# A graph layer and a state-space block on one core: the decay matrix from two single-pass products, a copy and a normalisation moved to ScalarE

## The chip, the cores and the metric

The kernel runs on one core of a Trainium2 chip. The core has five engines that run side by side and meet only through semaphores: TensorE (PE, matrix products; PEld is its loading of weights), VectorE (DVE), ScalarE (ACT), GpSimd (POOL) and SyncE (SP, which issues the DMAs here). The metric is the device time of one execution in microseconds. Three runs of the kernel before gave 901.51, 902.1 and 906.42 us; 902.1 is the median.

## The reference, cut to what matters

The input is x (4096 rows of 128) with an adjacency matrix of 4096 x 4096. A graph layer comes first: a masked softmax over the neighbours, two products with it, and a residual. Then a state-space block runs over the 4096 rows in 32 chunks of 128 rows, with 4 heads:

```python
x = x + _L0_gnn_ref(_layernorm(x), h0, a, temp, adj, 1)
x = x + _L0_ffn_ref(_layernorm(x)[None], W_in, conv_w, ...)[0]
# inside the block
z, xBC, dt = jnp.split(x @ W_in, ...)
xBC = jax.nn.silu(conv)                        # 4 taps, 384 channels
xh, Bmat, Cmat = jnp.split(xBC, [256, 320])    # B and C: 64 channels each
dt = jax.nn.softplus(dt + dt_bias);  A = -jnp.exp(A_log)
dA = dtc * A                                   # one number per row and head
Lmat = jnp.exp(segsum(dA))                     # decay matrix, 128 x 128 per head
Y_diag = jnp.einsum('bcln,bcsn,bhcls,bcshp->bclhp', Cc, Bc, Lmat, xdt)
...
Y = Y * jax.nn.silu(z);  Y = Y * rsqrt(mean(Y * Y) + EPS) * norm_w
out = (Y @ W_out) @ W_lin + b_lin
```

The change is about three values in it: the sums of dA inside the exponential of Lmat, the matrix C, and the layernorm in front of the block.

## The kernel before, in words

The program has two halves. The first reads the adjacency matrix, turns it into codes of one byte, makes two 0/1 masks of it (mask A on ScalarE, mask C on VectorE) and multiplies them with Y on TensorE. The second half reads the codes back, makes the masks again for the second product, and runs the state-space block beside it. The functions named slot below are that second half.

There is one slot function for each engine, and schedule calls it 37 times: 32 row tiles and 5 more calls in which the pipeline runs empty. In slot s an engine works on five different tiles at once. ok[0] is the end of the graph layer for tile s-1 and its layernorm, ok[1] the input projection and the convolution of tile s-2, ok[2] the decay matrix of tile s-3, ok[3] the outputs and the state of tile s-4, and ok[4] the storing of tile s-5. The order within an engine is the order of the code; across engines only the semaphores count. A helper named link lets an engine wait for its own last instruction before it goes on.

What the lines do, in the second half:
- VectorE: L691 is a pass that makes mask C from codes, four in each slot (mask(0) to mask(3)). L838 and L852 make the mixing matrix, L858 the output row tile (it waits for rs_ready, from GpSimd's L592), L862 and L867 the tile x1 after the graph layer, L880 and L905 its mean and variance. L895 are the nine convolution taps, between which the small steps of the softplus stand. L912 is the layernorm itself (normalise2), L921, L924 and L930 read the products of the state step, L967 gives dA to GpSimd, L976, L982 and L985 are the gates, and L986 makes a second copy of C, moved to partitions 0 to 63.
- GpSimd: L562 and L563 add epsilon and take the power -0.5 for the layernorm. L566 and L542 to L550 are six instructions of 128x128 on residuals. L573 multiplies the triangle upto with dA, which gives dam (128 x 4 x 128). L581, L583 and L585 scale x and the state. L591 and L592 are epsilon and power for the last norm, rs_ready.
- TensorE: L1283 and L1293 are the products with the masks, eight instructions of 256 columns each in a block. L1421 multiplies the triangle after with dam, 512 columns in fp32; after is exactly 0 or 1. L1377 transposes the normalised tile.
- ScalarE: L1053 makes mask A, L1072 reads the accumulator, L1152 copies the turned tile, L1165 are the first products of the convolution, L1183 is the tanh of it.

## Time and profile before

| | |
|---|---|
| runs, us | 901.51, 902.1, 906.42 |
| the profiled execution, us | 900.56 |
| its span, first to last instruction, us | 898.8 |
| mean granted TensorE clock | 0.957 |
| busy: PE, PEld, DVE | 818.9 (91%), 767.0 (85%), 792.5 (88%) |
| busy: ACT, POOL | 592.0 (66%), 543.9 (61%) |

The profiled execution took 900.56 us; its span is 898.8 us. Busy times are sums over the whole span, while the two halves have different limits, so they don't tell which engine sets the length of a slot. A slot is read from the distance between two executions of the same line. An instruction's time in the profile includes time in which it stands at its engine's head for something that is no semaphore.

### The profile page before, as it was taken

What the parts mean: (1) busy time and instruction counts of PE and PEld (TensorE: products, weight loads), DVE (VectorE), ACT (ScalarE), POOL (GpSimd) and SP (SyncE); (2) the same over time, 40 slices, a digit from 0 to 9 for tenths busy, and PEclk for the clock granted to TensorE, in tenths of its full rate; (3) what the DMA queues carried; (4) which work ended last, traced back from release to release, by engine and by line L of the source; (5) the groups of instructions that cost most, each with busy time, mean ns of one, the idle gap of its engine ahead of it and who ended that gap; (6) DMA issues with size and microseconds to landing.
All of it is one profiled execution on the core that took longest, in us unless ns stands there. A gap on an engine that the chain in (4) does not pass through costs nothing.

```text
span 898.8 us, 21768 instructions
## 1 busy us (share of the span) xinstructions
PE 818.9 (91%) x6650; PEld 767.0 (85%) x6650; DVE 792.5 (88%) x1968; ACT 592.0 (66%) x1026; POOL 543.9 (61%) x1123
## 2 busy tenths in 40 slices
PE   3978999989998999955889999999999999999976
PEld 1668999989998999954889999999999999999954
DVE  6567999989998999657699999999999999999983
ACT  6676877778787887533566666666666666666641
POOL 4462556664655666788656666575665756666642
PEclk9878999999999999995899999999999999999997
DMA  6456978878696967700111112111121111110000
GB/s 190 141 187 196 286 254 267 266 215 280 206 306 195 308 206 258 224 3 24 36 60 62 50 50 66 36 61 58 38 64 35 61 58 41 61 36 16 7 7 10
DMA packets 97545, 110.72 MB, mean 123 GB/s; under 512 B 6464, under 2 KB 89280, under 8 KB 97472
## 3 DMA queue, kind: packets, MB, share of 16 engines
q1 hardware_dynamic: 97472, 109.74, 38.7%
q8 instruction: 46, 0.75, 0.4%
q14 instruction: 27, 0.22, 0.1%
HBM read 90.85 MB, written 18.87 MB: 122 GB/s over the span
## 4 chain that ended last, share of the span: by engine, by line
PE 40%; POOL 20%; issue 13%; DVE 12%; ACT 8%; DMA 5%; POOLq 1%; DVEq 1%; ACTq 0%; SPq 0%
PE accA L1283 12%; PE accC L1293 11%; DMA adj_in<-in_adj_dram 5%; ACT edges L1006 3%; PE ps L1223 3%; PE ps L1421 2%; DVE maskC L691 2%; PE ps L1401 2%; PE ps L1399 2%; ACT maskA L1053 2%; DVE code L683 2%; POOL small L471 2%; DVE code L895 1%; PE ps L1403 1%; POOL featsum L490 1%
## 5 line engine op out<-in xcount | busy, mean ns | idle before, releaser
L1283 PE MATMUL accA<-Y,maskA 128*128 128x260 f32 (+1 forms) x2048 | 313.8, 296 | 30.5 <-DVE Y L662 19.1
L1053 ACT ACTIVATE maskA<-code 128x1024 fp32r<-128x1024 int8 x256 | 269.3, 1053 | 56.6 <-PE accC L1293 28.3
L1283 PEld LDWEIGHTS accA<-Y,maskA 128*128 128x128 f32 x2048 | 270.0, 193 | 33.7 <-ACT maskA L1053 16.9
L1293 PE MATMUL accC<-Y,maskC 128*128 128x260 f32 (+1 forms) x2048 | 295.3, 288 | 1.1 <-DVE maskC L691 1.1
L1293 PEld LDWEIGHTS accC<-Y,maskC 128*128 128x128 f32 x2048 | 268.4, 194 | 1.4 <-DVE maskC L691 1.4
L683 DVE SCALAR_TENSOR_TENSOR code<-f_rows,neg_f,ps 128x512 int8<-128x512 f32 x256 | 178.4, 740 | 37.1 <-PE ps L1223 35.5
L691 DVE TENSOR_SCALAR maskC<-code 128x1024 fp32r<-128x1024 int8 x256 | 210.0, 824 | 1.2 <-issue 0.3
L1006 ACT ACTIVATE edges<-adj_in 128x1024 bf16<-128x1024 f32 x128 | 133.1, 1044 | 24.5 <-DMA adj_in<-in_adj_dram 16.4
L895 DVE SCALAR_TENSOR_TENSOR code<-adj_in,f_rows,code 128x128 f32<-128x128 f32 x288 | 113.7, 415 | 0.0
L1223 PE MATMUL ps<-ident,edges 128*128 128x128 bf16 x1024 | 82.5, 225 | 13.3 <-ACT edges L1006 9.8
L1223 PEld LDWEIGHTS ps<-ident,edges 128*128 128x128 bf16 x1024 | 60.7, 101 | 24.1 <-DVE code L683 8.0
L562 POOL TENSOR_TENSOR f_rows<-f_rows,consts 128x1 f32<-128x1 f32 x32 | 8.4, 263 | 118.6 <-DVE f_rows L905 118.6
L573 POOL TENSOR_TENSOR f_rows<-f_rows 128x512 f32<-128x512 f32 x32 | 39.1, 1220 | 31.6 <-DVE f_rows L967 30.4
L462 POOL COPY small<-roww 128x2 f32 (+1 forms) x32 | 6.3, 198 | 83.2 <-DVE ps_sum L709 81.4
L1201 ACT COPY adj_in<-ps 128x256 f32<-128x256 f32 x32 | 12.0, 375 | 49.6 <-PE ps L1433 49.6
L1160 ACT COPY code<-ps 128x260 f32<-128x260 f32 x32 | 12.0, 376 | 48.7 <-PE ps L1388 48.7
L1183 ACT ACTIVATE code<-code 128x384 f32<-128x384 f32 x32 | 16.8, 525 | 35.6 <-DVE code L895 35.6
L1165 ACT ACTIVATE code<-ps,f_rows 128x128 f32<-128x128 f32 x96 | 37.5, 474 | 0.0
L581 POOL TENSOR_TENSOR adj_in<-code,f_rows 128x256 f32<-128x256 f32 x32 | 32.2, 1006 | 7.2 <-ACT code L1190 7.2
L1401 PE MATMUL ps<-adj_in,code 128*128 128x64 f32 x256 | 36.5, 266 | 0.0
L1421 PE MATMUL ps<-f_rows 128*128 128x512 f32 x64 | 36.0, 646 | 0.0
L1399 PE MATMUL ps<-adj_in,code 128*128 128x128 f32 x128 | 30.0, 317 | 6.2 <-DVE code L852 5.4
(201 smaller groups left out, 1487.3 us busy)
## 6 DMA issues: line engine op xcount, KB each, us to landing
adj_in<-in_adj_dram SPq DMA_DIRECT2D x128, 512.0 KB, 4.6
edge_codes<-code SPq DMA_DIRECT2D x8, 2048.0 KB, 10.0
code<-edge_codes SPq DMA_DIRECT2D x32, 512.0 KB, 3.3
xn<-in_x_dram SPq DMA_DIRECT2D x4, 512.0 KB, 5.8
adj_in<-in_x_dram SPq DMA_DIRECT2D x32, 64.0 KB, 1.8
adj_in<-in_L_gnn_h_dram SPq DMA_DIRECT2D x32, 64.0 KB, 1.9
out_dram<-adj_in SPq DMA_DIRECT2D x32, 64.0 KB, 1.6
f_rows<-in_L_ffn_W_in_dram SPq DMA_DIRECT2D x1, 192.0 KB, 6.6
```

Of the source, the lines that this page charges most:

```text
L573: g.tensor_tensor(dam, upto.unsqueeze(1).broadcast_to([P, NH, P]), tiny[:, 2 + k % 2, NH:2 * NH].unsqueeze(2).broadcast_to([P, NH, P]), AL ...
L683: v.scalar_tensor_tensor(out=code[:, par, :, jt * P:(jt + 1) * P], in0=f1_rows[:, rows].rearrange("p (i r) -> p i r", i=IT), scalar=neg_f2 ...
L691: v.tensor_scalar(maskC[:, b % MASKS], src, 2.0, None, ALU.is_equal).then_inc(S["maskC_ready"], 1)
L895: ins = v.scalar_tensor_tensor(out=conv[:, cb], in0=hist[:, k2, cb, tap:tap + P], scalar=conv_wt[:, cb, tap:tap + 1], in1=conv[:, cb], op0 ...
L1006: s.activation(edges[:, h % 4], adj_in[:, h % 4], ACT.Sign).then_inc(S["signed"], 1)
L1053: s.activation(maskA[:, b % MASKS], src, ACT.Relu, bias=-2.0).then_inc(S["maskA_ready"], 1)
L1223: m = t_.matmul(ps[jt % TRB][:, it * P:(it + 1) * P], edges[:, b % 4, it, j * P:(j + 1) * P], ident2[:], start=True, stop=True)
L1283: t_.matmul(accA[k][:, 0:2 * cols], maskA[:, b % MASKS, l * P:(l + 1) * P], Y[:, jt, 0, :, 0:cols], start=jt == 0, stop=jt == NT - 1)
L1293: m = t_.matmul(accC[k][:, 0:2 * cols], maskC[:, b % MASKS, l * P:(l + 1) * P], Y[:, jt, 1, :, 0:cols], start=jt == 0, stop=jt == NT - 1)
L1399: t_.matmul(ps[0][:, kb * P:(kb + 1) * P], xbc[:, (k - 4) % 2, kb, :], skip_w[:, kb], start=True, stop=False)
L1401: t_.matmul(ps[0][:, h * HD:(h + 1) * HD], wmix[:, h], xdt[:, h * HD:(h + 1) * HD], start=False, stop=h == (kb + 1) * P // HD - 1)
L1421: t_.matmul(ps[3][:, 0:NH * P], after, dam.rearrange("p h w -> p (h w)"), start=True, stop=True)
```

## The change

Four edits:
1. The decay matrix. dA = dt * A is split on GpSimd into a part that is rounded to fp32r and the rest. dam becomes two matrices of 4 x 128 columns, written by one instruction of 1024 elements, of type fp32r. TensorE sums two fp32r products of 512 columns in place of one fp32 product of 512. The matrices lie in the room that the tile edges of the first half had.
2. The second copy of C is made on ScalarE, from the finished xbc at the head of the next slot, in place of VectorE's L986. TensorE's product with it waits for the new semaphore cT_ready.
3. The layernorm in front of the block is one activation on ScalarE behind mask(2), x * rstd + bias, in place of VectorE's L912.
4. GpSimd makes the bias for it, -mean * rstd, in one more instruction, with a link ahead.

```diff
--- before.py
+++ after.py
@@ -66,7 +66,9 @@
             return ctx.enter_context(nc.psum_tensor(name, shape, dt))
 
         adj_in = sb("adj_in", [P, 4, IT, JH * P])
-        edges = sb("edges", [P, 4, IT, 2 * P], BF16)
+        with nc.sbuf_tensor("edges", [P, 4, IT, 2 * P], BF16) as edges:
+            pass
+        edge_room = sb("edge_room", [P, 4 * IT * P], F32R)
         code = sb("code", [P, 2, IT, NT * P], I8)
         maskA = sb("maskA", [P, MASKS, JB * P], F32R)
         maskC = sb("maskC", [P, MASKS, JB * P], F32R)
...
@@ -186,7 +188,9 @@
         ztan = y_space.take(DI)
         cT = rows_space.take(2, P)
         gate = rows_space.take(2, DI)
-        dam = rows_space.take(NH, P)
+        dam = edge_space.take(2, NH, P)
+        after = edge_space.take(P)
+        da_parts = edge_space.take(2, NH)
         expD = code_space.take(NH, P)
         gm = adj_space.take(P)
         wmix = code_space.take(NH, P)
...
@@ -560,7 +564,8 @@
                     wait(pool, "ln_done", s_)
                     wait(pool, "xn2_ready", s_ - 1)
                     link(g.tensor_tensor(tiny[:, 1, 0:1], tiny[:, 0, 1:2], consts[:, 2, 0:1], ALU.add))
-                    g.tensor_tensor(tiny[:, 1, 1:2], tiny[:, 1, 0:1], consts[:, 0, 0:1], ALU.pow).then_inc(S["rstd2"], 1)
+                    link(g.tensor_tensor(tiny[:, 1, 1:2], tiny[:, 1, 0:1], consts[:, 0, 0:1], ALU.pow))
+                    g.tensor_scalar(tiny[:, 1, 2:3], tiny[:, 0, 0:1], tiny[:, 1, 1:2], -1.0, ALU.mult, ALU.mult).then_inc(S["rstd2"], 1)
 
                     wait(pool, "out_done", s_ - 4)
                     g.tensor_tensor(x1b[:, kt], x1[:, kt % 2], b_row, ALU.add).then_inc(S["x1b_done"], 1)
...
@@ -570,8 +575,12 @@
 
                     wait(pool, "dt_ready", s_ - 1)
                     wait(pool, "p_cum", s_ - 2)
-                    g.tensor_tensor(dam, upto.unsqueeze(1).broadcast_to([P, NH, P]),
-                                    tiny[:, 2 + k % 2, NH:2 * NH].unsqueeze(2).broadcast_to([P, NH, P]), ALU.mult).then_inc(S["dam_ready"], 1)
+                    da = tiny[:, 2 + k % 2, NH:2 * NH]
+                    link(g.tensor_tensor(da_parts[:, 0], tiny[:, 2 + k % 2, 0:NH], a_row, ALU.mult))
+                    link(g.tensor_tensor(da_parts[:, 1], da, da_parts[:, 0].bitcast(F32), ALU.subtract))
+                    g.tensor_tensor(dam.rearrange("p a h w -> p (a h) w"), upto.unsqueeze(1).broadcast_to([P, 2 * NH, P]),
+                                    da_parts.rearrange("p a h -> p (a h)").bitcast(F32).unsqueeze(2).broadcast_to([P, 2 * NH, P]),
+                                    ALU.mult).then_inc(S["dam_ready"], 1)
                 if ok[2]:
 
                     kc = (k - 3) % 2
...
@@ -904,13 +913,6 @@
                     dve.wait_ge(S["vch"], seen)
                     v.bn_aggr(tiny[:, 0, 0:2], tiny[:, 7, 0:6]).then_inc(S["ln_done"], 1)
 
-                def normalise2():
-
-                    if ok[0]:
-                        dve.wait_ge(S["rstd2"], s_)
-                        wait(dve, "p_xT", s_ - 2)
-                        v.tensor_scalar(xn2[:, kt], x1[:, kt], tiny[:, 0, 0:1], tiny[:, 1, 1:2], ALU.subtract, ALU.mult).then_inc(S["xn2_ready"], 1)
-
                 summed_y = [0]
 
                 def y_state():
...
@@ -982,9 +982,8 @@
                     v.scalar_tensor_tensor(out=gate[:, k2], in0=ztan, scalar=1.0, in1=zdt[:, 0:DI], op0=ALU.add, op1=ALU.mult).then_inc(S["gate_done"], 1)
                     dve.wait_ge(S["ctan_ready"], s_ - 1)
                     wait(dve, "p_y", s_ - 3)
-                    v.scalar_tensor_tensor(out=xbc[:, k2], in0=gate_t, scalar=1.0, in1=conv, op0=ALU.add, op1=ALU.mult)
-                    v.scalar_tensor_tensor(out=cT[0:DS, k2], in0=gate_t[DS:P, CB - 1], scalar=1.0, in1=conv[DS:P, CB - 1], op0=ALU.add,
-                                           op1=ALU.mult).then_inc(S["conv_ready"], 1)
+                    wait(dve, "cT_ready", s_ - 3)
+                    v.scalar_tensor_tensor(out=xbc[:, k2], in0=gate_t, scalar=1.0, in1=conv, op0=ALU.add, op1=ALU.mult).then_inc(S["conv_ready"], 1)
                 mask(3)
                 end_chain()
 
...
@@ -1145,6 +1144,11 @@
 
                 if ok[0]:
                     read_acc(s_ - 1, (k - 1) % 2, F, 1)
+                if ok[2]:
+
+                    act.wait_ge(S["conv_ready"], s_ - 2)
+                    wait(act, "p_y", s_ - 4)
+                    s.copy(cT[0:DS, (k - 3) % 2], xbc[DS:P, (k - 3) % 2, CB - 1]).then_inc(S["cT_ready"], 1)
                 if ok[1]:
 
                     act.wait_ge(S["p_xT"], s_ - 1)
...
@@ -1177,6 +1181,10 @@
                     act.wait_ge(S["zcopy"], s_ - 1)
                     s.activation(ztan, zdt[:, 0:DI], ACT.Tanh).then_inc(S["zt_ready"], 1)
                 mask(2)
+                if ok[0]:
+                    act.wait_ge(S["rstd2"], s_)
+                    wait(act, "p_xT", s_ - 2)
+                    s.activation(xn2[:, (k - 1) % 2], x1[:, (k - 1) % 2], ACT.Identity, bias=tiny[:, 1, 2:3], scale=tiny[:, 1, 1:2]).then_inc(S["xn2_ready"], 1)
                 if ok[1]:
                     act.wait_ge(S["conv_pre"], s_ - 1)
                     wait(act, "conv_ready", s_ - 2)
...
@@ -1418,7 +1426,8 @@
                     pe.wait_ge(S["conv_ready"], s_ - 2)
                     t_.matmul(ps[2][:, 0:NH], upto, da, start=True, stop=True)
                     t_.matmul(ps[2][:, NH:2 * NH], ones[:], da, start=True, stop=True)
-                    t_.matmul(ps[3][:, 0:NH * P], after, dam.rearrange("p h w -> p (h w)"), start=True, stop=True)
+                    for half in range(2):
+                        t_.matmul(ps[3][:, 0:NH * P], after, dam[:, half].rearrange("p h w -> p (h w)"), start=half == 0, stop=half == 1)
                     for cb in range(CB):
                         m = t_.transpose(ps[2][:, (cb + 1) * P:(cb + 2) * P], xbc[:, c3, cb], ident[:])
                     m.then_inc(S["p_cum"], 1)
...
@@ -1437,6 +1446,7 @@
                 if ok[2]:
 
                     pe.wait_ge(S["conv_ready"], s_ - 2)
+                    pe.wait_ge(S["cT_ready"], s_ - 2)
                     if ok[3]:
                         pe.wait_ge(S["st_done"], s_ - 3)
                     t_.matmul(ps[1][:, 0:P], xbc[:, (k - 3) % 2, CB - 1, :], cT[:, (k - 3) % 2], start=True, stop=True).then_inc(S["p_g"], 1)
```

GpSimd's order around the decay matrix in a full slot, before (edge_room is the new room, f_rows holds upto, dA and other small tiles):

```order
L550 TENSOR_TENSOR adj_in<-featw 128x128
L573 TENSOR_TENSOR f_rows<-f_rows 128x512
L581 TENSOR_TENSOR adj_in<-code,f_rows 128x256
L583 TENSOR_TENSOR f_rows<-adj_in,code 128x256
L585 TENSOR_TENSOR ywork<-code,f_rows 64x256
L591 TENSOR_TENSOR f_rows<-f_rows,consts 128x1
L592 TENSOR_TENSOR f_rows<-f_rows,consts 128x1
L392 ISA
L562 TENSOR_TENSOR f_rows<-f_rows,consts 128x1
L563 TENSOR_TENSOR f_rows<-f_rows,consts 128x1
L566 TENSOR_TENSOR adj_in<-adj_in,f_rows 128x128
```

The same place of GpSimd in the changed file:

```order
L554 TENSOR_TENSOR adj_in<-featw 128x128
L579 TENSOR_TENSOR edge_room<-f_rows 128x4
L580 TENSOR_TENSOR edge_room<-f_rows,edge_room 128x4
L581 TENSOR_TENSOR edge_room<-f_rows,edge_room 128x1024
L590 TENSOR_TENSOR adj_in<-code,f_rows 128x256
L592 TENSOR_TENSOR f_rows<-adj_in,code 128x256
L594 TENSOR_TENSOR ywork<-code,f_rows 64x256
L600 TENSOR_TENSOR f_rows<-f_rows,consts 128x1
L601 TENSOR_TENSOR f_rows<-f_rows,consts 128x1
```

Two small instructions stand ahead of the matrix now, and it is twice as wide; what follows it keeps its order (L581 to L592 are now L590 to L601). The instruction L568, behind the power, is the one of edit 4.

VectorE's order from the last small step of the softplus to the end of the slot, before:

```order
L958 TENSOR_TENSOR f_rows<-f_rows 128x4
L912 TENSOR_SCALAR adj_in<-adj_in,f_rows 128x128
L921 TENSOR_TENSOR ywork<-ps,f_rows 128x256
L924 TENSOR_TENSOR code<-ywork,ps 64x256
L964 SCALAR_TENSOR_TENSOR f_rows<-f_rows 128x4
L930 TENSOR_TENSOR ywork<-ywork,ps 128x256
L967 TENSOR_TENSOR f_rows<-f_rows 128x4
L976 TENSOR_TENSOR f_rows<-ywork,f_rows 128x256
L691 TENSOR_SCALAR maskC<-code 128x1024
L982 SCALAR_TENSOR_TENSOR f_rows<-ywork,code 128x256
L985 SCALAR_TENSOR_TENSOR code<-code 128x384
L986 SCALAR_TENSOR_TENSOR f_rows<-code 64x128
```

The same place of VectorE in the changed file:

```order
L960 TENSOR_TENSOR f_rows<-f_rows 128x4
L923 TENSOR_TENSOR ywork<-ps,f_rows 128x256
L926 TENSOR_TENSOR code<-ywork,ps 64x256
L965 SCALAR_TENSOR_TENSOR f_rows<-f_rows 128x4
L932 TENSOR_TENSOR ywork<-ywork,ps 128x256
L968 TENSOR_TENSOR f_rows<-f_rows 128x4
L976 TENSOR_TENSOR f_rows<-ywork,f_rows 128x256
L700 TENSOR_SCALAR maskC<-code 128x1024
L982 SCALAR_TENSOR_TENSOR f_rows<-ywork,code 128x256
L986 SCALAR_TENSOR_TENSOR code<-code 128x384
L700 TENSOR_SCALAR maskC<-code 128x1024
```

The layernorm and the copy of C are gone from it, and all else stands as before. L858 of the kernel before is L867 in the changed file.

## Rows read from the trace of the kernel before

**Rows 1.** Busy us by stage: engines with instruction counts, granted clock, DMA share, GB/s.

```profile
300.00:400.00 100.00, 93.27 (x869) 91.02 (x867) 79.98 (x148) 65.69 (x73) 68.27 (x187) 1.00 0.62 196
600.00:700.00 100.00, 99.49 (x765) 93.29 (x764) 98.46 (x282) 65.14 (x151) 63.13 (x109) 1.00 0.17 54
```

**Rows 2.** VectorE in order of time, one slot: start, duration, line, operation, idle.

```profile
610.72 0.18 DVE L905 BATCH_NORM_AGGREGATE f_rows<-f_rows 128x2 f32<-128x6 f32 x1
...
614.36 0.52 DVE L912 TENSOR_SCALAR adj_in<-adj_in,f_rows 128x128 f32<-128x128 f32 x1
...
616.32 1.54 DVE L691 TENSOR_SCALAR maskC<-code 128x1024 fp32r<-128x1024 int8 x1
617.78 0.83 DVE L982 SCALAR_TENSOR_TENSOR f_rows<-ywork,code 128x256 f32<-128x256 f32 x1
618.53 0.97 DVE L985 SCALAR_TENSOR_TENSOR code<-code 128x384 f32<-128x384 f32 x1
619.51 0.61 DVE L986 SCALAR_TENSOR_TENSOR f_rows<-code 64x128 f32<-64x128 f32 x1
620.15 0.69 DVE L691 TENSOR_SCALAR maskC<-code 128x1024 fp32r<-128x1024 int8 x1
...
622.55 0.34 DVE L858 SCALAR_TENSOR_TENSOR adj_in<-ps,f_rows,adj_in 128x128 f32<-128x128 f32 x1
...
624.63 0.17 DVE L905 BATCH_NORM_AGGREGATE f_rows<-f_rows 128x2 f32<-128x6 f32 x1
```

**Rows 3.** GpSimd in order of time, same slot.

```profile
610.97 0.28 POOL L562 TENSOR_TENSOR f_rows<-f_rows,consts 128x1 f32<-128x1 f32 x1 [3.64 <-DVE f_rows L905]
611.33 0.55 POOL L563 TENSOR_TENSOR f_rows<-f_rows,consts 128x1 f32<-128x1 f32 x1
...
616.09 1.22 POOL L573 TENSOR_TENSOR f_rows<-f_rows 128x512 f32<-128x512 f32 x1 [0.75 <-DVE f_rows L967]
617.27 1.06 POOL L581 TENSOR_TENSOR adj_in<-code,f_rows 128x256 f32<-128x256 f32 x1
...
620.25 1.00 POOL L592 TENSOR_TENSOR f_rows<-f_rows,consts 128x1 f32<-128x1 f32 x1
624.89 0.28 POOL L562 TENSOR_TENSOR f_rows<-f_rows,consts 128x1 f32<-128x1 f32 x1 [3.64 <-DVE f_rows L905]
```

**Rows 4.** GpSimd in order of time: first and last of 26 slots, one later row.

```profile
495.07 1.01 POOL L592 TENSOR_TENSOR f_rows<-f_rows,consts 128x1 f32<-128x1 f32 x1
...
842.83 1.00 POOL L592 TENSOR_TENSOR f_rows<-f_rows,consts 128x1 f32<-128x1 f32 x1
...
887.12 0.62 POOL L581 TENSOR_TENSOR adj_in<-code,f_rows 128x256 f32<-128x256 f32 x1 [7.18 <-ACT code L1190]
```

**Rows 5.** Waits between 560 and 860 us: who for whom, total, times, longest.

```profile
POOL f_rows L562 <- DVE f_rows L905: 79.5, 22, 3.8
...
ACT code L1183 <- DVE code L895: 22.4, 21, 2.0
POOL f_rows L573 <- DVE f_rows L967: 16.9, 22, 0.8
```

**Rows 6.** VectorE in order of time, an early slot.

```profile
452.44 1.26 DVE L982 SCALAR_TENSOR_TENSOR f_rows<-ywork,code 128x256 f32<-128x256 f32 x1
453.62 0.54 DVE L985 SCALAR_TENSOR_TENSOR code<-code 128x384 f32<-128x384 f32 x1
```

**Rows 7.** TensorE in order of time, same slot as rows 2.

```profile
612.76 1.11 PE L1421 MATMUL ps<-f_rows 128*128 128x512 f32 x2
...
613.95 1.20 PE L1283 MATMUL accA<-Y,maskA 128*128 128x256 f32 x8
```

**Rows 8.** ScalarE's groups by form, whole span: count, busy, mean ns, idle before.

```profile
L1165 ACT ACTIVATE code<-ps,f_rows 128x128 f32<-128x128 f32 x96 | 37.5, 474 | 0.0
```

**Rows 9.** GpSimd's groups by form, whole span.

```profile
L433 POOL TENSOR_TENSOR Y<-code,Y 128x1024 fp32r<-128x1024 f32 x2 | 4.7, 2355 | 2.6 <-ACT Y L1042 2.6
L501 POOL TENSOR_TENSOR ywork<-xn,colw 128x1024 f32<-128x1024 f32 x1 | 1.9, 1900 | 0.4 <-POOL row_out L484 0.4
```

More of the change, by code:

```diff
@@ L146, in gnn_ffn_kernel @@
         y_space = Space(ywork[:, :])
+        edge_space = Space(edge_room[:, :])
         DI = W_out.shape[0]
@@ L169, in gnn_ffn_kernel @@
         upto = rows_space.take(P)
-        after = rows_space.take(P)
         x_in = adj_space.take(2, F)
@@ L217, in gnn_ffn_kernel @@
             mix_ready xdt_ready  ps_ready y_read yg_ready st_done skip_ready yT_ready ssq_ready rs_ready
-            exp_done out_done zcopy""".split()
+            exp_done out_done zcopy cT_ready""".split()
         S = {n: sem(n) for n in names}
@@ L958, in slot @@
                     last = step(v.tensor_tensor(p, horner[:, 2, :, 5], si, ALU.mult))
-                    normalise2()
                     y_state()
@@ L968, in slot @@
                 else:
-                    normalise2()
                     y_state()
```

## The prediction

> **What bounds the kernel now.** I first read the table by stage. In the second half of the program (the state-space block beside the second products) TensorE is busy 99.49 of 100 us and VectorE 98.46, while GpSimd shows 63.13; in the first half TensorE has 93.27 and VectorE 79.98 [rows 1]. The change touches nothing in the first half, so everything below is about the slots of the second. Their length is the distance of two equal instructions: L905 at 610.72 and 624.63 on VectorE, L562 at 610.97 and 624.89 on GpSimd [rows 2, 3], so 13.92 us. There are 26 such full slots: L592 runs from 495.07 to 842.83 in 26 executions, 25 distances of 13.91 [rows 4].
>
> Then I read the order in time of one slot on each engine, because three engines are near the limit and GpSimd, with 63% busy, looks free but is not. Every slot holds a loop: L905 (statistics of the new row tile) releases GpSimd's L562; GpSimd works through to L592, the norm factor of an older tile; L592 releases VectorE's L858, and from L858 VectorE goes on, in its own order, to the next L905. In numbers: L905 ends at 610.90, L592 ends at 621.25, L858 starts at 622.55 and the next L905 ends at 624.80 [rows 2, 3]. So GpSimd's part is 10.35 us (0.75 of it is L573 waiting for VectorE's step size L967), the slack between L592 and L858 is 1.30, and VectorE's part is 2.25. GpSimd's 3.64 us of idle time before L562 are not free time: 2.25 + 0.10 of them are this loop's VectorE part, and only 1.30 is slack. The list of waits says the same: 79.5 us over 22 slots are L562 waiting for L905, and 16.9 are L573 waiting for L967 [rows 5].
>
> The third reading is that VectorE and GpSimd take turns. A mask pass L691 takes 0.69 us at 620.15 but 1.54 at 616.32, where it ends 0.55 after L573 (0.55 being most of a pass) [rows 2, 3]. L982 takes 0.83 beside L581, and 1.26 in an early slot; L985 takes 0.97 in the full slot, and 0.54 where GpSimd stands still [rows 2, 6]. The other way round, L581 takes 1.06 behind the mask pass and 0.62 without it [rows 3, 4], and the power L592 takes 1.00 behind the mask pass of 620.15, while the same power in L563 takes 0.55. Each of these is explained by one engine standing for the other's whole instruction and then running at its normal speed. The Trainium skill (SBUF — State Buffer, "Who interferes with whom") states this: GpSimd shares a port pair with VectorE, as an exclusive lock held for a whole instruction, against VectorE instructions with two SBUF inputs or in a two-port mode. The trace agrees, by the 1.54 against 0.69. By that rule of the Trainium skill a longer GpSimd instruction is paid on both engines, which speaks against this change: without turns the slot would be rival 1's 13.4, with them it is what is worked out below from rows.
>
> **The change part by part.**
> TensorE: L1421's product goes from fp32 to two fp32r products of 512 columns. L1421 now shows two records and 1.11 us; eight fp32r products of 256 columns take 1.20 [rows 7], so two of 512 cost as much as four of those, 0.60 at most. Removed: 0.5 us per slot. TensorE alone would then allow a slot of 13.4.
>
> VectorE: L912 (0.52) and L986 (0.61) go [rows 2]; instructions overlap by 0.08, so 1.0 to 1.05 us. But by the next part some of this is waiting for GpSimd, which what stands behind them would do in their place; I take 0.6 as sure.
>
> ScalarE: gets a copy of 64x128 and an activation of 128x128. The nearest row, L912 on VectorE, has 0.52 for the latter; ScalarE does its conv activations L1165, of the same size, in a mean of 0.47 [rows 8]. Together at most 1.0 us on an engine that is 65% busy [rows 1]; L1183 alone waits 22.4 us in 21 slots [rows 5], and the activation is placed just ahead of it. Cost 0 while that second is there; without it at most 0.5. The normalised tile is wanted by TensorE only at the head of the next slot, and the copy of C most of a slot after it is made, so both new waits are covered. Behind the copy's wait in ScalarE's queue stands the copy of the turned tile; it may be 0.5 late, and its taker, TensorE, has by then gained that.
>
> GpSimd, per slot:
> - L568 in the changed file, 128x1, with a link ahead of it: L562 of that size takes 0.28, and 0.36 from start to start [rows 3]. I take 0.3.
> - two 128x4 instructions with links ahead of the matrix: 0.3 each by the same row, 0.6.
> - the matrix from 512 to 1024 elements. 1.22 now [rows 3]. A 1024 element instruction with one spread operand took 1.90; one with two full operands and an fp32r output 2.36 [rows 9]. So it grows by 0.68 to 1.14; I take 0.9, as the rows with spread operands are nearer in form and the 1.22 holds a short wait for L976.
> - the 0.75 us wait for L967 is used up: the step size comes some 0.4 earlier (L912 is gone) and GpSimd 0.3 later.
> Sum: 10.35 - 0.75 + 0.3 + 0.6 + 0.9 = 11.4 us. The room up to L858 is 11.65. So with the turns as they are, the loop would not bind at all, by 0.25.
>
> The turns are what decides. Now GpSimd stands for VectorE about 1.4 us per slot: 0.44 in L581, 0.45 in L592, the rest in L573 and L585. Going through the slot with the rule "whoever asks first holds for its whole instruction", and the undisturbed times 0.69, 0.54, 0.62, 0.55 and 1.90, I let the new instructions come at their new places: L568 shifts GpSimd's five small row instructions against the convolution taps L895, the two 128x4 instructions each meet the mask pass L691 or L982, and L581, L583, L585 come one mask pass later. That gives 0.5 to 1.0 us of waits more than now. With 0.75 the GpSimd part is 12.15, so L858 starts 0.5 later than now: a slot of 14.4 us. VectorE then idles ahead of L858 and TensorE about 1.0 us per slot. TensorE's clock should stay: in a stretch with 93.27% busy the granted clock was 1.00 [rows 1].
>
> Early slots gain (VectorE and TensorE bind them), by at most 0.5 each for three slots; the last slots, where nothing runs beside the block, lose about as much in GpSimd's longer stretch. I put them at 0. Total: 26 x 0.5 = +13 us on a profiled time of 900.56 (span 898.8), so 913.6; the median of the runs is 902.1, 1.5 above the profiled one, so **915**.
>
> **The rivals.**
> 1. Turns cost nothing more, or VectorE's gain absorbs them. For it: 11.4 is under 11.65. Then VectorE (13.92 - 0.6) and TensorE (13.4) bind, a slot of 13.4 to 13.5: 26 x -0.48 = -12.5, **889.5**. Against it: three more instructions have to take turns.
> 2. Slack and new waits cancel, slot 13.8 to 14.05: **902**, within 4 us.
> 3. The GpSimd loop binds harder: the matrix at the 2.36 of rows 9 and 1.0 us of waits or more, slot 14.9 to 15.2: about 26 x 1.25, **934**. Its place is L858 waiting for L592; it decides from a GpSimd part of 12.6.
> 4. The split product isn't cheap: if fp32r products of 512 columns cost what the fp32 ones do, TensorE gets +0.94 or more per slot, slot 14.9, +24, **926**. Against it: the rate of the eight products in rows 7.
>
> **How the numbers follow.** Forecast (slot 14.2 to 14.8) 0.48, its own range 908 to 924; rival 1 0.27; rival 2 0.12; rival 3 0.10; rival 4 0.03. A measurement here can tell 0.5%, 4.5 us, from no change. Slower: 0.48 + 0.10 + 0.03 = 0.61; same 0.12; faster 0.27. The range 889 to 928 leaves out most of rival 3 and the edge of rival 1.
>
> **What would show it.** Right: VectorE's L858 (L867 in the changed file) waits for GpSimd's power in every full slot, 0.3 to 1.4 us, where it now starts 1.30 behind it; slots of 14.2 to 14.8; TensorE below 97% in the second half; the matrix at 1.9 to 2.4 us; VectorE's instructions beside it up to 2 us long. ScalarE's two additions wait for nobody that matters. Wrong: slots under 13.9 with L867 starting at once would mean that the turns were over-counted; slots over 15 that the matrix or the turns were under-counted; a wait of TensorE's L1385 or L1394 for ScalarE would mean that I wrongly costed the moved normalisation or copy at nothing.

## The result and the profile after

The changed kernel took 938.0 us (median of 4 runs, 937.16 to 939.79), the kernel before 902.88 beside it (4 runs, 901.51 to 906.42): 1.038 of it, interval 1.034 to 1.042. It is slower, as forecast, but by 35 us where 13 were forecast, and outside the range of 889 to 928. The span of its profiled execution is also 938.0 us (898.8 before), the mean granted clock there 0.940 (0.957). The two profiled executions lie 39 us apart, the medians 35.

The table by stage, with the columns of [rows 1]:

```profile
300.00:400.00 100.00, 95.65 (x892) 93.33 (x890) 80.74 (x150) 67.59 (x75) 69.05 (x188) 1.00 0.65 204
600.00:700.00 100.00, 90.93 (x706) 86.76 (x706) 82.86 (x234) 64.95 (x152) 75.96 (x118) 0.99 0.14 45
```

Between 300 and 400 us, in the first half, little changes. In the second, TensorE falls from 99.49 to 90.93 and VectorE from 98.46 to 82.86, and GpSimd rises from 63.13 to 75.96. The granted clock stays at the upper level there (0.99). One slot of the changed kernel on GpSimd, in order of time (start, duration, line, operation, idle time before and who ended it), answers to [rows 3]:

```profile
625.33 0.28 POOL L566 TENSOR_TENSOR f_rows<-f_rows,consts 128x1 f32<-128x1 f32 x1 [2.38 <-DVE f_rows L914]
625.69 0.55 POOL L567 TENSOR_TENSOR f_rows<-f_rows,consts 128x1 f32<-128x1 f32 x1
626.34 0.47 POOL L568 TENSOR_SCALAR f_rows<-f_rows 128x1 f32<-128x1 f32 x1
626.77 0.60 POOL L571 TENSOR_TENSOR adj_in<-adj_in,f_rows 128x128 f32<-128x128 f32 x1
...
630.37 0.79 POOL L554 TENSOR_TENSOR adj_in<-featw 128x128 f32<-128x128 f32 x1
631.40 0.57 POOL L579 TENSOR_TENSOR edge_room<-f_rows 128x4 fp32r<-128x4 f32 x1 [0.24 <-POOL adj_in L554]
632.05 0.52 POOL L580 TENSOR_TENSOR edge_room<-f_rows,edge_room 128x4 fp32r<-128x4 f32 x1
632.65 1.91 POOL L581 TENSOR_TENSOR edge_room<-f_rows,edge_room 128x1024 fp32r<-128x1024 f32 x1
634.52 1.06 POOL L590 TENSOR_TENSOR adj_in<-code,f_rows 128x256 f32<-128x256 f32 x1
...
637.40 0.55 POOL L601 TENSOR_TENSOR f_rows<-f_rows,consts 128x1 f32<-128x1 f32 x1
640.44 0.28 POOL L566 TENSOR_TENSOR f_rows<-f_rows,consts 128x1 f32<-128x1 f32 x1 [2.48 <-DVE f_rows L914]
```

VectorE in the same slot, answering to [rows 2]:

```profile
625.07 0.18 DVE L914 BATCH_NORM_AGGREGATE f_rows<-f_rows 128x2 f32<-128x6 f32 x1
...
633.32 1.79 DVE L861 TENSOR_TENSOR code<-code,adj_in 128x512 f32<-128x512 f32 x1
635.04 1.10 DVE L700 TENSOR_SCALAR maskC<-code 128x1024 fp32r<-128x1024 int8 x1
638.09 0.35 DVE L867 SCALAR_TENSOR_TENSOR adj_in<-ps,f_rows,adj_in 128x128 f32<-128x128 f32 x1 [1.96 <-POOL f_rows L601]
...
640.18 0.17 DVE L914 BATCH_NORM_AGGREGATE f_rows<-f_rows 128x2 f32<-128x6 f32 x1
```

The slot is 15.11 us here, 15.07 in the mean (13.91 before, counted in the same way: 25 distances of the power's line). All mean slots below are counted so. The output instruction L867 stands 1.96 us for GpSimd's power L601; before it started 1.30 behind it. From the start of the statistics to the end of that power it is 12.88 us (10.53 before): I call this the stretch. The waits between 560 and 860 us (who for whom: total, times, longest) say the same of all slots:

```profile
POOL f_rows L566 <- DVE f_rows L914: 49.5, 20, 2.7
DVE adj_in L867 <- POOL f_rows L601: 37.3, 20, 2.0
PEld ps L1407 <- issue: 27.4, 18, 1.6
```

GpSimd waits for VectorE and VectorE for GpSimd in every slot: the loop of the prediction now binds from both sides. The third line is TensorE standing ahead of the products with the mixing matrix. The profile names nobody for it; in the code they also wait for GpSimd's scaling L592, and in this slot they start at 636.71, 0.11 behind its end.

Who lost turns has changed as well. The nine convolution taps are one group in the page (line, operation, count | busy, mean ns | idle before); before the same group had 113.7 us in all and a mean of 415 ns:

```profile
L904 DVE SCALAR_TENSOR_TENSOR code<-adj_in,f_rows,code 128x128 f32<-128x128 f32 x288 | 91.6, 338 | 0.0
```

VectorE's taps no longer stand for GpSimd. GpSimd's row instructions (the seven of 128x128, L571 and L546 to L554 here) stand for VectorE instead, three at 0.60 and the last at 0.79 in the slot above.

Where the 39.2 us of span went: 26 full slots times 1.15 are 29.9; the ramp up and one more slot 3.1; the time from the last statistics (894.31, before 859.48) to the end grew from 39.3 to 43.7, 4.4; and the first statistics come 1.8 later.

Most of the 4.4 us at the end is TensorE's clock. From the transposes of the last tile (L1433 at 887.75, here L1442 at 923.72) to the end of the span it is 11.05 us before and 14.28 here, with the same work in it. The same product, first before, then after:

```profile
891.84 0.65 PE L1403 MATMUL ps<-code,f_rows 128*128 128x256 f32 x2
929.79 1.17 PE L1411 MATMUL ps<-code,f_rows 128*128 128x256 f32 x2
```

The granted clock is 1.00 from 890 to 896 us before (the upper level, 2.4 GHz) and 0.50 from 926 to 932 us here (1.2 GHz). Shortly ahead of this both show 0.50 (879 to 884 us before, 914 to 923 here); why it came back in the one and not in the other, no run here separates. In the last 12 us the profile of act_only shows 0.89, as the kernel before does (0.88), and the profiles of all other runs 0.50 to 0.64, so up to 3 us of their distance from the kernel before lie there and not in the slots.

### The profile page after: what moved, and what is told of

It reads as the page before. It is cut to its first block, busy times and chain, and to the rows that moved or that the text cites. A ratio compares the mean times of both kernels' runs of the same rounds, so it can differ in the third digit from the quotient of the medians.

```text
span 938.0 us, 21890 instructions
## 1 busy us (share of the span) xinstructions
PE 826.4 (88%) x6650; PEld 782.2 (83%) x6650; DVE 760.6 (81%) x1904; ACT 617.8 (66%) x1090; POOL 627.1 (67%) x1219
## 4 chain that ended last, share of the span: by engine, by line
POOL 41%; issue 18%; PE 17%; DVE 11%; ACT 6%; DMA 4%; POOLq 1%; DVEq 1%; ACTq 0%; SPq 0%
PE accA L1291 5%; PE accC L1301 5%; DMA adj_in<-in_adj_dram 3%; POOL adj_in L590 3%; POOL f_rows L592 3%; ACT edges L1005 3%; PE ps L1231 2%; POOL adj_in L554 2%; POOL small L475 2%; POOL ywork L594 2%; POOL adj_in L571 2%; DVE code L904 2%; POOL featw L547 2%; POOL featw L553 2%; POOL f_rows L567 2%
## 5 line engine op out<-in xcount | busy, mean ns | idle before, releaser
L1291 PE MATMUL accA<-Y,maskA 128*128 128x260 f32 (+1 forms) x2048 | 319.8, 300 | 29.9 <-DVE Y L671 18.2
L1291 PEld LDWEIGHTS accA<-Y,maskA 128*128 128x128 f32 x2048 | 275.5, 197 | 33.4 <-ACT maskA L1052 19.8
L1301 PEld LDWEIGHTS accC<-Y,maskC 128*128 128x128 f32 x2048 | 271.4, 196 | 1.6 <-DVE maskC L700 1.4
L700 DVE TENSOR_SCALAR maskC<-code 128x1024 fp32r<-128x1024 int8 x256 | 204.9, 805 | 0.3 <-issue 0.3
L904 DVE SCALAR_TENSOR_TENSOR code<-adj_in,f_rows,code 128x128 f32<-128x128 f32 x288 | 91.6, 338 | 0.0
L581 POOL TENSOR_TENSOR edge_room<-f_rows,edge_room 128x1024 fp32r<-128x1024 f32 x32 | 62.2, 1944 | 2.5
L1178 ACT ACTIVATE f_rows<-f_rows 128x4 f32<-128x4 f32 x32 | 6.6, 207 | 80.6 <-DVE f_rows L936 80.6
L1407 PEld LDWEIGHTS ps<-adj_in,code 128*128 128x128 f32 x128 | 21.1, 207 | 44.3 <-issue 42.9
L867 DVE SCALAR_TENSOR_TENSOR adj_in<-ps,f_rows,adj_in 128x128 f32<-128x128 f32 x32 | 11.2, 350 | 57.5 <-POOL f_rows L601 57.4
L861 DVE TENSOR_TENSOR code<-code,adj_in 128x512 f32<-128x512 f32 x32 | 51.2, 1601 | 0.1
```

What stands on the lines that cost most here:

```text
L581: g.tensor_tensor(dam.rearrange("p a h w -> p (a h) w"), upto.unsqueeze(1).broadcast_to([P, 2 * NH, P]), da_parts.rearrange("p a h -> p (a ...
L700: v.tensor_scalar(maskC[:, b % MASKS], src, 2.0, None, ALU.is_equal).then_inc(S["maskC_ready"], 1)
L861: v.tensor_tensor(wmix, expD, gm.unsqueeze(1).broadcast_to([P, NH, P]), ALU.mult).then_inc(S["mix_ready"], 1)
L904: ins = v.scalar_tensor_tensor(out=conv[:, cb], in0=hist[:, k2, cb, tap:tap + P], scalar=conv_wt[:, cb, tap:tap + 1], in1=conv[:, cb], op0 ...
L1291: t_.matmul(accA[k][:, 0:2 * cols], maskA[:, b % MASKS, l * P:(l + 1) * P], Y[:, jt, 0, :, 0:cols], start=jt == 0, stop=jt == NT - 1)
L1301: m = t_.matmul(accC[k][:, 0:2 * cols], maskC[:, b % MASKS, l * P:(l + 1) * P], Y[:, jt, 1, :, 0:cols], start=jt == 0, stop=jt == NT - 1)
```

## The experiments

The theory after the result: the loop through the wait for the power binds, and it is lengthened by the port turns that the added small GpSimd instructions (bias, two parts) cause, more than by the twice as wide matrix. (This last part did not hold for the time; see both_off.) Rivals: the matrix alone; ScalarE's additions; VectorE as the bound. All ratios are to the kernel before, from three rounds each, with the interval. Line numbers in rows are those of each run's own file; the order changes are written in short, not as code.

**One edit, or the others.** split_only is the kernel before with edit 1 alone:

```diff
+ link(g.tensor_tensor(da_parts[:, 0], tiny[:, 2 + k % 2, 0:NH], a_row, ALU.mult))
+ link(g.tensor_tensor(da_parts[:, 1], da, da_parts[:, 0].bitcast(F32), ALU.subtract))
- g.tensor_tensor(dam, ...)                        # 4 x 128
+ g.tensor_tensor(dam.rearrange(...), ...)         # 2 x 4 x 128, fp32r
```

> The kernel before with edit 1 alone (the split decay matrix: two 128x4 instructions, 1024 columns on GpSimd, two fp32r products). Theory L (the loop: GpSimd's stretch from VectorE's statistics to the power of the last norm, then VectorE's output instruction and back to the statistics, sets the slot): the stretch grows by 0.6 + 0.7 us and by turns, slot 14.6 to 15.2, 920 to 938 us. Rival S (what costs is on ScalarE: the moved copy and normalisation come late for TensorE): with these left out the time would fall below the kernel before, to some 890 us, by the cheaper products. Rival V (VectorE itself is slowed by the long GpSimd instruction, whatever waits for the power): also 920 to 940.

act_only is the changed kernel with these lines taken back (edits 2 to 4 alone).

> The changed kernel with edit 1 undone: copy of C and normalisation on ScalarE, the bias instruction on GpSimd, decay matrix as before (512 columns, one fp32 product). Theory L: GpSimd's stretch is about 11 us and fits the room, TensorE bounds with its old work, slot 13.9, 898 to 905 us. Rival S: keeps most of the loss, 925 to 938. Rival V: VectorE has 0.6 us less to do, but TensorE bounds, 898 to 905.

split_only: 924.22 us, 1.021 (1.017 to 1.025), slots of 14.53, stretch 12.37, a time within the expected 920 to 938. act_only: 900.95 us, 0.995 (0.992 to 0.998), slots of 13.94, stretch 11.75. Alone they are worth +2.1% and -0.5%, together +3.8%: they don't add. GpSimd in a slot of split_only:

```profile
610.84 0.46 POOL L554 TENSOR_TENSOR adj_in<-featw 128x128 f32<-128x128 f32 x1
612.05 0.37 POOL L578 TENSOR_TENSOR edge_room<-f_rows 128x4 fp32r<-128x4 f32 x1 [0.76 <-DVE f_rows L975]
...
617.90 1.13 POOL L600 TENSOR_TENSOR f_rows<-f_rows,consts 128x1 f32<-128x1 f32 x1
```

and VectorE's output instruction there, and in act_only:

```profile
619.07 0.35 DVE L866 SCALAR_TENSOR_TENSOR adj_in<-ps,f_rows,adj_in 128x128 f32<-128x128 f32 x1
```

```profile
623.26 0.35 DVE L859 SCALAR_TENSOR_TENSOR adj_in<-ps,f_rows,adj_in 128x128 f32<-128x128 f32 x1 [1.38 <-POOL f_rows L593]
```

In split_only the row part ends before the step size is there (it still waits 0.76 at L578), and the output follows directly behind the power: the edit alone used up all of the 1.30 of slack. act_only uses it up too, and waits. With both, the second user has no slack left. So act_only's time came true for another reason than the expected one (a stretch of about 11 that fits the room): the time was luck. Rival S is out by split_only, which has no addition on ScalarE and still loses 2.1%.

**The low half left out.** high_only keeps one part, a matrix of 512 and one product, so dA is only its rounded value:

```diff
- g.tensor_tensor(dam.rearrange("p a h w -> p (a h) w"), ...)
+ g.tensor_tensor(dam[:, 0], ...)
```

> The changed kernel with the low part of dA left out: one 128x4 instruction, a matrix of 512 fp32r columns, one fp32r product of 512 columns (so the decay matrix is computed from rounded values). Theory L: the stretch is shorter by 0.6 + 0.9 us, slot 13.6 to 14.1, 893 to 908 us. Rival V: about the same, 895 to 910. Rival S: 925 to 938, since nothing changes on ScalarE.

904.09 us, 0.998 (0.996 to 1.001), slots of 13.96, stretch 11.78, as expected by the loop and by rival V alike. The matrix took 1.37 (1.91 after). VectorE in one slot:

```profile
621.04 0.68 DVE L859 TENSOR_TENSOR code<-code,adj_in 128x512 f32<-128x512 f32 x1
...
624.71 0.35 DVE L865 SCALAR_TENSOR_TENSOR adj_in<-ps,f_rows,adj_in 128x128 f32<-128x128 f32 x1 [1.96 <-POOL f_rows L599]
```

The mixing matrix takes 0.68 here and 1.79 (L861) in the changed kernel, and yet the output waits the same 1.96: VectorE standing for GpSimd ahead of a wait costs nothing, it is only waited out at another place. The loop's length counts, and with 1.10 less of it the slot is 1.11 shorter.

**The matrix last.** dam_last is the changed kernel with GpSimd's order scalings (L590 to L594 of the changed kernel), norm (L600, L601), then the two parts and the matrix.

```diff
- if ok[1]: parts, matrix   if ok[2]: scalings   if ok[3]: norm
+ if ok[2]: scalings   if ok[3]: norm   if ok[1]: parts, matrix
```

> The changed kernel with one order changed on GpSimd: in each slot the scalings and the two instructions of the last norm come ahead of the decay matrix and its two small instructions, which then are the last of the slot. No instruction more or less. Theory L: the power is ready 3 us earlier, the output instruction waits for nothing, and the slot falls to what TensorE needs (13.4 to 13.7), 887 to 897 us. Rival V: VectorE meets the same GpSimd work, only elsewhere, 925 to 940. Rival G (GpSimd has too much work in all, in whatever order): 12.7 us of stretch plus turns, also at or above 14.5, 920 to 938.

910.13 us, 1.007 (1.004 to 1.009), slots of 14.12. That is 28 us better than the changed kernel, but not the 887 to 897 expected, and no gain over the kernel before. VectorE:

```profile
623.48 0.35 DVE L867 SCALAR_TENSOR_TENSOR adj_in<-ps,f_rows,adj_in 128x128 f32<-128x128 f32 x1 [0.54 <-POOL f_rows L591]
...
624.17 1.78 DVE L876 SCALAR_TENSOR_TENSOR adj_in<-ywork,row_out,adj_in 128x128 f32<-128x128 f32 x1
```

The wait is still 0.54, and now L876, in VectorE's own part of the loop, takes 1.78 instead of 0.35: it stands for the 1.93 us matrix. A wide GpSimd instruction moved off one half of the loop landed on the other. This is rival V's mechanism, though not its 925 to 940: the stretch fell to 10.47, and VectorE's part, from the output to the next statistics, rose from 2.1 to 3.5.

**One small instruction.** one_more is the kernel before with edit 4 alone; nobody reads the bias.

```diff
- g.tensor_tensor(tiny[:, 1, 1:2], ...pow).then_inc(S["rstd2"], 1)
+ link(g.tensor_tensor(tiny[:, 1, 1:2], ...pow))
+ g.tensor_scalar(tiny[:, 1, 2:3], ...).then_inc(S["rstd2"], 1)
```

> The kernel before with one more small instruction on GpSimd: the bias of the layernorm, 128x1, with a link ahead of it, and nobody reads it. Nothing else is changed. Theory F (it shifts GpSimd against VectorE's convolution taps, so that the turns flip): the six row instructions of 128x128 behind it take some 0.60 us each where they took 0.44 to 0.49, the taps 0.34 where they took 0.55, and the last of the six ends about 6.0 us after the statistics' start where it ended at 4.6. The time stays, 898 to 906 us, since GpSimd's stretch had 1.3 us of room. Rival P (it costs its own duration only): the last of the six ends at 5.1 to 5.3, taps stay at 0.55, time the same.

915.9 us, 1.015 (1.009 to 1.020), slots of 14.6 in the middle of the run, stretch 12.38. For the first row instructions and the taps the expectation came true (0.60, a mean of 340 ns), for the time not: something else was hit. GpSimd and VectorE at the same moment:

```profile
623.15 0.60 POOL L542 TENSOR_TENSOR featw<-xn,row_out 128x128 f32 x1
...
626.12 2.00 POOL L550 TENSOR_TENSOR adj_in<-featw 128x128 f32<-128x128 f32 x1
```

```profile
625.98 0.41 DVE L977 TENSOR_TENSOR f_rows<-ywork,f_rows 128x256 f32<-128x256 f32 x1
626.32 0.68 DVE L692 TENSOR_SCALAR maskC<-code 128x1024 fp32r<-128x1024 int8 x1
626.92 0.41 DVE L983 SCALAR_TENSOR_TENSOR f_rows<-ywork,code 128x256 f32<-128x256 f32 x1
627.25 0.54 DVE L986 SCALAR_TENSOR_TENSOR code<-code 128x384 f32<-128x384 f32 x1
```

L550 (0.46 for its like in split_only) takes 2.00, while four VectorE instructions in a row run at their undisturbed times (0.68 and 0.54 are those the prediction used). GpSimd lost the port to all of them. By the rule I had used, it would have had its turn behind the first.

This is where the time went. In the first three full slots of this run and in the last three L550 is done in 0.60:

```profile
524.56 0.60 POOL L550 TENSOR_TENSOR adj_in<-featw 128x128 f32<-128x128 f32 x1
```

There the added instruction is in place and the first row instructions take 0.60 as well, and yet these slots last 13.66 to 13.88 us, no more than the same slots of the kernel before (13.72 to 13.95). In the 20 slots between, L550 takes 2.00 and the slot 14.4 to 14.7. So where L550 was not held up, the added instruction and the turned row instructions cost nothing; what cost was the turns that L550 lost. In the changed kernel the like of it, L554, takes 0.79.

**The bias off GpSimd.** bias_on_scalar is the changed kernel with L568 replaced by two small activations on ScalarE:

```diff
- g.tensor_scalar(tiny[:, 1, 2:3], ...)
+ s.mul(tiny[:, 1, 3:4], tiny[:, 0, 0:1], tiny[:, 1, 1:2])
+ s.activation(tiny[:, 1, 2:3], tiny[:, 1, 3:4], ACT.Identity, scale=-1.0)
```

> The changed kernel with edit 4 taken off GpSimd: ScalarE makes the bias in two small activations ahead of the moved normalisation. Theory F: GpSimd's row instructions keep their old turns, the stretch up to the power is about 12.3 us as in the kernel with edit 1 alone, slot 14.4 to 14.6, 917 to 926 us. Rival P: the stretch is only 0.5 shorter at most, slot 14.7 to 14.9, 927 to 934. Rival S (ScalarE's additions are what costs): 938 or more.

918.06 us, 1.016 (1.011 to 1.022), slots of 14.33 to 14.55, stretch 12.2, as theory F expected. GpSimd's row instructions are back at 0.40 to 0.49, and the output waits 0.44. One instruction on 128x1 was worth 20 us of the 35.

**The parts off GpSimd too.** both_off also makes the two 128x4 parts on VectorE, ahead of dt_ready (`v.tensor_tensor(da_parts[:, 0], ...)` and the same for the rest). both_off_mid then puts the norm's two instructions directly behind the matrix, ahead of the scalings.

> The changed kernel with three small instructions taken off GpSimd: the bias made by ScalarE as in bias_on_scalar, and the two 128x4 parts of dA by VectorE. GpSimd keeps the matrix of 1024 columns. Theory L with F: the stretch is 11.1 to 11.4 us, slot 13.4 to 13.7, which TensorE or the loop sets, 887 to 899 us. Rival V (the wide matrix alone, in VectorE's way, is the cost): the slot stays over 14.3, 915 or more.

> both_off with GpSimd's two instructions of the last norm placed directly behind the matrix, ahead of the scalings. Theory L: the output instruction waits for nothing any more and TensorE or VectorE sets the slot, 13.4 to 13.6, 886 to 896 us. Rival T (the scalings now meet VectorE's x1 instructions, which are on the loop too, as the matrix did in dam_last): no gain over both_off, or up to 8 us more than it.

both_off: 922.06 us, 1.022 (1.016 to 1.027); slots of 14.46 though the stretch was 11.35 and nothing waited for the power. My theory failed and rival V came true: VectorE was the bound. VectorE, and its stage:

```profile
609.95 2.40 DVE L696 TENSOR_SCALAR maskC<-code 128x1024 fp32r<-128x1024 int8 x1
612.27 0.83 DVE L982 SCALAR_TENSOR_TENSOR f_rows<-ywork,code 128x256 f32<-128x256 f32 x1
613.03 0.97 DVE L986 SCALAR_TENSOR_TENSOR code<-code 128x384 f32<-128x384 f32 x1
613.92 1.10 DVE L696 TENSOR_SCALAR maskC<-code 128x1024 fp32r<-128x1024 int8 x1
```

```profile
600.00:700.00 100.00, 95.28 (x734) 90.47 (x735) 98.64 (x272) 72.13 (x174) 66.14 (x104) 1.00 0.16 50
```

The mask pass stands 1.71 for the matrix, the three behind it about 0.4 each for the scalings: these four rows alone hold 3.0 us of standing in each slot, which the 98.64 counts as busy. So the matrix is not the smaller cost. The small instructions lengthen the stretch more than it does (1.25 for the two parts against 0.69 for its growth), but taking all three off GpSimd gives back 16 us, while leaving out half the matrix and one of them (high_only) gives back 34. both_off_mid: 904.14 us, 1.001 (0.998 to 1.003), slots of 13.78: 18 us better than both_off, which rival T had excluded, but short of the 886 to 896 expected. The 2.40 stayed, the 0.83 and 0.97 became 0.41 and 0.55.

**The norm early, in both kernels.** rs_mid is the changed kernel, before_rs_mid the kernel before, each with the norm's two instructions behind the matrix:

```diff
- if ok[1]: matrix   if ok[2]: scalings   if ok[3]: norm
+ if ok[1]: matrix   if ok[3]: norm   if ok[2]: scalings
```

> The changed kernel with GpSimd's two instructions of the last norm placed behind the decay matrix and ahead of the three scalings, nothing else. Theory L (the changed kernel's slot is set by the output instruction waiting for this power, 1.85 us): the power is ready some 2.5 us earlier, that wait goes, and VectorE or TensorE sets the slot: 13.6 to 14.1, 893 to 908 us. Rival V (VectorE's own queue, with what it waits for the port, is as long): 925 or more.

> The kernel before with the same reordering of GpSimd (norm's two instructions directly behind the decay matrix), as a control. Theory L: the power was already 1.30 us early, so nothing is won, 899 to 905 us. Rival: if the reordering helps by changing which turns are lost, the slot moves here too, by 0.3 us or more, to under 896 or over 910.

rs_mid: 911.03 us, 1.007 (1.004 to 1.010), slots of 13.92 in the mean, alternately some 13.76 and 14.06; its output instruction waits for nobody:

```profile
624.90 0.34 DVE L867 SCALAR_TENSOR_TENSOR adj_in<-ps,f_rows,adj_in 128x128 f32<-128x128 f32 x1
```

With all of the changed kernel's work in place, moving the power forward takes back 27 of the 35 us. Some 5 of these are the reorder's own gain, by the control below; the rest shows that the wait for the power carried most of the loss. The slot is within the 13.6 to 14.1 expected, the time 3 us above the 893 to 908. TensorE's wait for the scalings did not set the changed kernel's slot: they come later here, and the kernel is faster. What sets the 13.92 here, half a microsecond above TensorE's 13.4, no run separates. before_rs_mid is the control: 899.44 us, 0.994 (0.991 to 0.997), slots of 13.60. I had expected nothing, since nothing waited for the power there; the time is inside the expected range, but the slot moved by 0.31, which was the rival's sign. VectorE, beside [rows 2]:

```profile
618.01 0.41 DVE L982 SCALAR_TENSOR_TENSOR f_rows<-ywork,code 128x256 f32<-128x256 f32 x1
618.34 0.55 DVE L985 SCALAR_TENSOR_TENSOR code<-code 128x384 f32<-128x384 f32 x1
618.90 0.29 DVE L986 SCALAR_TENSOR_TENSOR f_rows<-code 64x128 f32<-64x128 f32 x1
```

0.83, 0.97 and 0.61 became 0.41, 0.55 and 0.29: the order of GpSimd's queue alone changed who stands for whom.

**A version that beats both.** half_on_scalar is both_off with the high half of the matrix made by four ScalarE activations, and only the low half (512) on GpSimd; half_on_scalar_mid also has the norm behind that half.

```diff
+ for h in range(NH):
+     m = s.mul(dam[:, 0, h], upto, da_parts[:, 0, h:h + 1].bitcast(F32))
- g.tensor_tensor(dam.rearrange("p a h w -> p (a h) w"), ...)
+ g.tensor_tensor(dam[:, 1], ...)
```

> both_off with the high half of the decay matrix made by ScalarE (four activations of 128x128 in its wait ahead of the softplus exponential) and only the low half, 512 columns, by GpSimd. Theory T (what both_off lost is VectorE standing for the long matrix and for turns behind it): the mask pass beside the matrix goes back to about 1.5 us, the slot to 13.4 to 13.7, which TensorE sets, 886 to 899 us. Rival S (ScalarE's additions now come late): the slot is 13.9 or more, with waits of TensorE or VectorE for ScalarE, 902 to 915.

> half_on_scalar with the two instructions of the last norm directly behind the low half on GpSimd. Theory T: the same as half_on_scalar or up to 4 us better, 884 to 899 us. Rival S: 902 to 915.

894.71 us, 0.989 (0.983 to 0.995), slots of 13.61, and 893.6 us, 0.986 (0.980 to 0.991), slots of 13.47. Both are as theory T expected, and the mask pass beside the matrix takes 1.54 again. The stage of the second:

```profile
600.00:700.00 100.00, 99.58 (x789) 95.77 (x787) 96.64 (x284) 83.16 (x212) 67.65 (x111) 1.00 0.17 52
```

TensorE is at 99.58 again, with more instructions in the 100 us than before (789, before 765), so its saved half microsecond per slot does arrive once GpSimd no longer holds it up. The interval of half_on_scalar_mid overlaps that of half_on_scalar, so what the last step adds is not settled.

## Why the prediction was wrong

Direction and mechanism held: slower, by the loop statistics, GpSimd's part, power L601, output L867, statistics. What it said would mean "the matrix or the turns were under-counted", slots over 15, is what came. The slot and the wait are rival 3's (14.9 to 15.2, GpSimd part from 12.6; measured 12.70), by its waits and not by its matrix of 2.36, which took 1.91; the time, 938 against its 934, even more.

By the terms of its sum, per slot:
- **The turns: the step that failed.** It had three small instructions at 0.9 us of their own and 0.75 of turns for all. In the trace the row part of GpSimd ends 6.09 behind the statistics in place of 4.62: +1.47, where L568 was priced at 0.3. The two 128x4 cost 1.25 from start to start, where 0.6 stood, since each takes 0.5 in place of 0.2 (0.20 is what dam_last shows for them). The scalings and the norm together got 0.55 shorter (3.98 before, 3.43 after). Net of the times priced for them that is 1.17 + 0.65 - 0.55 = 1.27 of turns where the sum had 0.75. These 0.52 are nearly the whole miss of 0.55 in GpSimd's part, 12.70 against 12.15 (the 0.24 of waiting left over and the 0.21 that the matrix cost less about cancel). L867 starts 1.19 later in its slot, against 0.5 forecast: 0.55 by this, and 0.14 by the distance from the power's end to L867's start, which the sum left out. bias_on_scalar confirms the largest item by taking L568 out, -20 us. one_more, with L568 put into the kernel before, loses 13 us, but by another victim, L550.
- **Why it came out at 0.5 to 1.0:** I let the engines alternate, whoever asks first. As I read the rows, each turn of 0.3 to 0.6 us depends on a shift of a few tenths in who asks first, and L568 turned the row instructions from those that hold the port (taps at 0.55) into those that stand for it. And an engine can lose several turns in a row, as L550 did. The Trainium skill (SBUF — State Buffer, "Who interferes with whom") states the exclusive lock for a whole instruction. The trace agrees: a mask pass of 0.69 is seen as 1.10, 1.54 and 2.40. The alternation was mine.
- **The matrix:** +0.9 forecast, +0.69 measured (1.87 from start to next, 1.18 before). Its own time is 1.91, the value of the spread-operand row. Right.
- **The 0.75 of waiting for the step size:** 0.24 is left, by the link behind L554. Right to 0.2.
- **TensorE:** two fp32r products take 0.54 from start to next, before 0.94: -0.40 (forecast -0.5). Right, and worth nothing while the loop binds.
- **ScalarE:** the copy takes 0.30, the normalisation 0.48, and neither is waited for with any weight. Right.
- **VectorE's gain of 0.6:** it arrived and was waited out ahead of L867.
- **Ramp and drain at 0:** wrong. 3.1 and 4.4 us, plus 1.8 at the first statistics, a quarter of the loss in the profiled executions. At the end 3.2 of the 4.4 are TensorE's products at the lower clock, for which the prediction had no term (it said that the clock should stay, and in the slots it did, 0.99); only the other 1.1 can be GpSimd's longer part. What the 3.1 consist of stays open.

The chances: the loop not binding (rivals 1 and 2) had 0.39, because 11.4 stood against a room of 11.65. act_only shows that even without the matrix and the two parts the room was used up. 11.4 was not a neutral middle: every term of GpSimd's sum had been taken at its undisturbed duration, and only one term stood for all disturbance.

What stays open: what decides who gets the port when both wait. In one_more GpSimd's L550 loses to three VectorE instructions that came after it; in both_off four VectorE instructions one behind the other each lose a turn to GpSimd. I found no rule that forecasts both. Nor do the runs split the 35 us cleanly between the longer stretch and VectorE standing for the wide matrix: rs_mid, which frees the output from the wait, gives back 27, and both_off, which shortens the stretch by 1.5, gives back 16.

## What to carry to other kernels

An engine with 63% busy can be the bound if it stands in a loop with another; count slack in the loop, not idle time, and ask of each edit how much of the same slack it takes. Small instructions on GpSimd beside a full VectorE are to be priced at what they take with the port contested (0.5 us here), and a single such instruction may turn over who stands for whom in the rest of the slot, so such a change is tried alone before it is bundled. Where a power or another small result is awaited by the neighbour, its place in the queue can be worth more than its duration.

## What the runs showed that I had not expected

- One GpSimd instruction of 128x1, with no reader, costs 1.5% of the kernel (ratio 1.015), and in its trace the longer slots are just those in which another GpSimd instruction loses its turns.
- The order alone, with the same instructions, moves the changed kernel by 27 us and the kernel before by 5.
- Where VectorE's output follows the power within 0.15 us and VectorE's own part is undisturbed, the slot is the stretch plus 2.2, in one slot each of six kernels: 11.75 and 13.98, 11.78 and 14.01, 12.21 and 14.33, 12.37 and 14.50, 12.38 and 14.61, 12.88 and 15.11. both_off, with 11.35 and 14.46, is where another bound took over.
- An fp32r output cost GpSimd nothing here: 1024 wide 1.91 with it, 1.90 without [rows 9]; 512 wide 1.20 with it (half_on_scalar), 1.22 without.
- The end of the last tile took 3.2 us more in one profile than in the other, with TensorE at the lower level of its clock in place of the upper.
